# Three groups of the feed-forward stage normalised at the end of the scan, the steepness test moved, and an unread state half left out

## The reference

```python
xn = layernorm(x, ln_w, ln_b)
z, xBC, dt = split(xn @ in_proj_w)
xBC = silu(causal_conv1d(xBC, conv_w, conv_b))       # four taps
# state of each head: h = h * exp(dt * A) + dt * x * B ;  y = h . C
y = ssd_scan(xh, softplus(dt + dt_bias), Bm, Cm, -exp(A_log)) + D_skip * xh
y = y * silu(z)
y = y * rsqrt(mean(y * y) + 1e-5) * rms_w
out = y @ out_proj_w + x
h = relu(layernorm(out) @ mlp_w1 + mlp_b1) @ mlp_w2 + mlp_b2
out = h + out
# second layer: router softmax, two of 8 experts a token, a capacity for each expert,
# silu(x @ W1 + b1) @ W2 + b2, gated and added back, with layernorms and residuals around
```

## Time and profile before

| | us |
|---|---|
| median of 3 runs | 875.31 |
| lowest, highest | 872.54, 875.57 |
| profiled execution, its own time | 874.87 |
| its span | 873.1 |
| PE, DVE, ACT, POOL busy | 709.1, 608.5, 490.8, 441.3 |

### The profile page before, as it was taken

One profiled execution on the slowest core, in us unless ns is written; L12 is line 12 of the kernel. 1 busy time (PEld: TensorE's weight loads), 2 busy tenths in 40 slices (PEclk: granted clock), 3 DMA queues, 4 the chain that ended last, 5 costly groups with the idle time before them and its releaser, 6 DMA issues. The chain is left out here.

```text
span 873.1 us, 14642 instructions
## 1 busy us (share of the span) xinstructions
PE 709.1 (81%) x3872; PEld 492.4 (56%) x3872; DVE 608.5 (70%) x2176; ACT 490.8 (56%) x1209; POOL 441.3 (51%) x576
## 2 busy tenths in 40 slices
PE   7657999999999997999999840055698878879994
PEld 3325667777777775698989730023454444444542
DVE  7957999999999993799999888897111211121168
ACT  4864666666667675687877426334243432334257
POOL 7603767667667664233433530000757777777500
PEclk8877999999999998999999955555699998999997
DMA  9930000000000000600000004000322212221197
GB/s 220 382 132 20 1 2 2 2 1 1 2 1 2 2 2 9 186 1 2 2 2 1 2 0 196 0 0 8 94 64 72 75 50 74 75 75 47 40 355 223
DMA packets 50414, 52.92 MB, mean 61 GB/s; under 512 B 7576, under 2 KB 39624, under 8 KB 50080
## 3 DMA queue, kind: packets, MB, share of 16 engines
q1 hardware_dynamic: 44496, 41.62, 14.6%
q0 software_dynamic: 5120, 10.37, 4.2%
q10 hardware_dynamic: 720, 0.05, 0.1%
HBM read 28.04 MB, written 24.18 MB: 60 GB/s over the span
## 5 line engine op out<-in xcount | busy, mean ns | idle before, releaser
L917 DVE SCALAR_TENSOR_TENSOR s_cv<-s_pU,tap_w,s_cv 128x256 f32<-128x256 f32 x372 | 153.4, 477 | 11.1 <-ACT s_cv L848 10.7
L1939 POOL DMA_INDIRECT arena<-token_rows,token_of x80 | 81.1, 1014 | 115.3 <-issue 114.7
L2060 DVE TENSOR_TENSOR arena<-e_pB,e_gate 128x384 f32<-128x384 f32 (+2 forms) x24 | 14.5, 602 | 122.5 <-PE e_pB L1984 122.5
L1947 POOL DMA_INDIRECT choice_rows<-arena,choice_of x80 | 79.6, 995 | 32.9 <-issue 22.6
L2011 ACT ACTIVATE e_h<-e_pH,e_bcols 128x384 f32<-128x384 f32 (+2 forms) x96 | 58.7, 616 | 65.4 <-PE e_pH L1968 63.0
L1968 PE MATMUL e_pH<-e_xgT,e_w 128*128 128x384 f32 (+2 forms) x192 | 82.7, 580 | 0.0
L716 POOL TENSOR_TENSOR s_xa<-s_xt,arena 128x512 f32<-128x512 f32 x32 | 34.4, 1074 | 86.9 <-ACT s_xt L866 86.9
L848 ACT ACTIVATE s_cv<-s_pU,tap_b,tap_w 128x256 f32<-128x256 f32 x124 | 63.5, 560 | 23.3 <-PE s_pU L750 23.0
L750 PE MATMUL s_pU<-arena,w_in 128*128 128x262 f32 x248 | 68.2, 399 | 8.4 <-DVE s_cv L917 3.9
L1976 PE MATMUL e_pO<-e_h,e_w 128*128 128x384 f32 (+2 forms) x192 | 72.7, 522 | 0.4 <-ACT e_oT L2018 0.4
L1492 PE MATMUL m_pM<-w_m,m_h 128*128 128x128 f32 x512 | 62.7, 276 | 0.1
(11 more groups left out here) (308 smaller groups left out, 1874.3 us busy)
## 6 DMA issues: line engine op xcount, KB each, us to landing
choice_rows<-zrow SPq DMA_DIRECT2D x16, 512.0 KB, 8.4
arena<-choice_rows SPq DMA_DIRECT2D x28, 256.0 KB, 5.1
token_rows<-arena SPq DMA_DIRECT2D x8, 520.0 KB, 5.8
n_x<-in_L_attn_x_dram SPq DMA_DIRECT2D x8, 512.0 KB, 7.5
arena<-in_L_attn_x_dram SPq DMA_DIRECT2D x8, 512.0 KB, 4.7
e_w<-in_L_ffn_W_dram SPq DMA_DIRECT2D x16, 256.0 KB, 3.1
out_dram<-arena SPq DMA_DIRECT2D x14, 256.0 KB, 4.2
decay_rows<-arena SPq DMA_DIRECT2D x2, 1024.0 KB, 4.7
```

Of the source, the lines that this page charges most:

```text
L917: v.scalar_tensor_tensor(out=by_tile(cv[:, p % 2, m, :]), in0=columns(m)[:, :, tap:tap + P], scalar=tap_w[:, m, tap:tap + 1], in1=by_tile( ...
L1939: g.indirect_dma_start(xg[:, n % RING, i, :], None, table, bass.IndirectOffsetOnAxis(ap=token_of[:, c:c + 1], axis=0), bounds_check=TOKENS ...
L1947: g.indirect_dma_start(choice, bass.IndirectOffsetOnAxis(ap=choice_of[:, c:c + 1], axis=0), yo[:, n % RING, i, :], None, bounds_check=2 * ...
```

## The change

A class `Opening` holds the residual sum, the statistics, the roots and the normalisation for the first three groups (`READY = 3`) with semaphores of its own. Its parts are called from the scan's queues: on ACT at lags 2 and 4 of the last pair, on DVE behind the staged list. The exact scan runs the same parts again in a second block at its end, since it writes `proj` and `ssq` anew. In the feed-forward stage the functions for the first normalisation return at once for those groups, and their semaphores are advanced by three at the start. The buffers that both stages use (`root_y`, `sd_y`, `m_h0`, `m_stats`, `m_mv`, `m_sd`, `m_rs`) move into spare columns of the tile `cv`, and `m_hn` is allocated for the whole kernel. The transposition of the extremes and the comparison move into the last pair's step. `add_b` returns at once for the last four pairs, `states` leaves the second bank out for them, and for the last three `states` waits for `carry_b` in the place of `add_b`.

```diff
+            def roots(self, a):
+                a.activation(sd_y[:, 0:G * READY], ssq[:, 0:G * READY], ACT.Sqrt, bias=eps[:, 0:1], scale=1.0 / INNER).then_inc(self.root, 1)
+            def deviation(self, a, g):
+                need(a, self.var, g)
+                a.activation(m_sd[:, 0, g], m_mv[:, 0, g, :, 1], ACT.Sqrt, bias=eps[:, 0:1]).then_inc(self.sd, 1)
+            def invert_roots(self, v):
+                v.wait_ge(self.root, 1)
+                v.reciprocal(root_y[:, 0:G * READY], sd_y[:, 0:G * READY]).then_inc(self.inverse, 1)
+                v.wait_ge(self.inverse, 1)
+            def residual(self, v, g):
+                for i in range(G):
+                    t = G * g + i
+                    ins = v.scalar_tensor_tensor(out=m_h0[:, g, i, :], in0=proj[:, t, :], scalar=root_y[:, t:t + 1], in1=res[:, g, i, :],
+                                                 op0=ALU.mult, op1=ALU.add)
+                ins.then_inc(self.h0, 1)
+                need(v, self.h0, g)
+                for i in range(G):
+                    ins = v.bn_stats(m_stats[:, 0, g, i, :], m_h0[:, g, i, :])
+                ins.then_inc(self.stat, 1)
+                need(v, self.stat, g)
+                for i in range(G):
+                    ins = v.bn_aggr(m_mv[:, 0, g, i, :], m_stats[:, 0, g, i, :])
+                ins.then_inc(self.var, 1)
+            def normal(self, v, g):
+                need(v, self.sd, g)
+                v.reciprocal(m_rs[:, 0, g], m_sd[:, 0, g]).then_inc(self.rs, 1)
+                need(v, self.rs, g)
+                for i in range(G):
+                    ins = v.tensor_scalar(m_hn[:, g, i, :], m_h0[:, g, i, :], m_mv[:, 0, g, i, 0:1], m_rs[:, 0, g, i:i + 1],
+                                          ALU.subtract, ALU.mult)
+                ins.then_inc(self.hn, 1)
+            def vector(self, v):
+                self.invert_roots(v)
+                for g in range(READY):
+                    self.residual(v, g)
+                    if g:
+                        self.normal(v, g - 1)
+                self.normal(v, READY - 1)
...
                 def states(p):
                     need(pe, s_bt, p)
                     need(pe, s_xa, p)
-                    need(pe, s_st, p, 1)
+                    if p <= PAIRS - BACK:
+                        need(pe, s_st, p, 1)
+                    else:
+                        need(pe, s_sb, p, 1)
                     for t in range(G2):
-                        for c in range(2):
+                        for c in range(2 if p < PAIRS - BACK else 1):
...
+                def far_row(p):
+                    if p == PAIRS - 1:
+                        pe.wait_ge(s_all, 1)
+                        need(pe, s_bt, p)
+                        pe.transpose(pTr[0:1, 0:P], farther[:, :], ident[:, :]).then_inc(s_row, 1)
                 staged([(0, project(0)), (0, project(1)), (3, outputs), (1, gram), (1, turn_x), (0, project(2)), (0, project(3)),
-                        (2, states), (1, turn_b), (4, turn_out), (2, project_z), (4, out_project)])
-                pe.wait_ge(s_all, 1)
-                need(pe, s_bt, PAIRS - 1)
-                pe.transpose(pTr[0:1, 0:P], farther[:, :], ident[:, :]).then_inc(s_row, 1)
+                        (2, states), (1, turn_b), (2, far_row), (4, turn_out), (2, project_z), (4, out_project)])
...
-                staged([(0, first_tap(0)), (0, first_tap(1)), (1, silu_b), (1, silu_c), (5, projected), (1, silu_x), (0, first_tap(2)),
-                        (0, first_tap(3)), (1, silu_bt), (4, turned), (4, squares), (2, silu_z), (2, residual_first)])
+                # open_roots, open_first, open_others: for the last pair alone, roots(a), deviation(a, 0), deviation(a, 1 and 2)
+                staged([(0, first_tap(0)), (0, first_tap(1)), (1, silu_b), (1, silu_c), (5, projected), (4, open_first), (1, silu_x),
+                        (0, first_tap(2)), (0, first_tap(3)), (1, silu_bt), (4, turned), (4, squares), (4, open_others), (2, silu_z),
+                        (2, residual_first), (2, open_roots)])
...
                 def add_b(p):
+                    if p >= PAIRS - BACK:
+                        return
...
-                staged([(0, extremes_of), (0, taps(0)), (1, mask), (3, scaled), (0, taps(2)), (2, add_a), (2, carry_b), (2, add_b)])
-                v.wait_ge(s_row, 1)
-                v.tensor_reduce(farthest[0:1, :], pTr[0:1, 0:P], AX.X, ALU.max).then_inc(s_all, 1)
-                v.wait_ge(s_all, 2)
-                v.tensor_scalar(steep[0:1, :], farthest[0:1, :], STEEP, None, ALU.is_gt).then_inc(s_all, 1)
+                def compared(p):
+                    if p == PAIRS - 1:
+                        v.wait_ge(s_row, 1)
+                        v.tensor_reduce(farthest[0:1, :], pTr[0:1, 0:P], AX.X, ALU.max).then_inc(s_all, 1)
+                        v.wait_ge(s_all, 2)
+                        v.tensor_scalar(steep[0:1, :], farthest[0:1, :], STEEP, None, ALU.is_gt).then_inc(s_all, 1)
+                staged([(0, extremes_of), (0, taps(0)), (1, mask), (3, scaled), (0, taps(2)), (2, add_a), (2, carry_b), (2, add_b),
+                        (2, compared)])
+                need(v, s_bs, PAIRS - 1)
+                need(v, s_cs, PAIRS - 1)
+                need(v, s_bt, PAIRS - 1)
+                need(v, s_o, READY - 1)
+                opening.vector(v)
...
+            def opened(g):
+                return isinstance(g, int) and g < READY
...
                 a.activation(sd_y[:, :], ssq[:, :], ACT.Sqrt, bias=eps[:, 0:1], scale=1.0 / INNER).then_inc(s_extra2, 1)
+                a.sem_inc(s_sd[0], READY)
...
+                for s_ in (s_h0, s_st[0], s_var[0], s_rs[0], s_hn):
+                    v.sem_inc(s_, READY)
                 v.wait_ge(s_extra2, 1)
```

More of the change, by code:

```diff
@@ L196, in build @@
         rev, enough, base = taken(EXPERTS), taken(4), taken(1)
+        NB, G, READY = 4, 2, 3
+        root_y, sd_y = taken(TILES), taken(TILES)
+        m_stats = taken(3 * NB * G * 6).rearrange("p (n k g s) -> p n k g s", n=3, k=NB, g=G)
+        m_mv = taken(3 * NB * G * 2).rearrange("p (n k g s) -> p n k g s", n=3, k=NB, g=G)
+        m_sd, m_rs = (taken(3 * NB * G).rearrange("p (n k g) -> p n k g", n=3, k=NB) for _ in range(2))
+        assert room[0] <= 1024
+        m_h0 = spare_room[:, 1024:2048].rearrange("p (k g d) -> p k g d", k=NB, g=G)
+        m_hn = sb("m_hn", [P, NB, G, D])
         same_half = sb("c_same_half", [P, P], F16)
@@ L625, in _, with __init__ @@
                 v.memset(state[:, :, :], 0.0)
+        class Opening:
+            def __init__(self, name):
+                self.root, self.inverse, self.h0, self.stat, self.var, self.sd, self.rs, self.hn = (
+                    nc.alloc_semaphore(name=name + n) for n in ("_root", "_inverse", "_h0", "_stat", "_var", "_sd", "_rs", "_hn"))
+            def roots(self, a):
[36 more added lines that the diff above has]
+                self.normal(v, READY - 1)
@@ L628, in build @@
+        opening, opening_again = Opening("fast"), Opening("slow")
         with ExitStack() as st:
@@ L904, in residual_first, with open_roots, open_first, open_others @@
                         a.activation(res[:, q, i, :], x_first[:, t, :], ACT.Identity, bias=minus_m[:, t:t + 1], scale=rstd[:, t:t + 1])
-                staged([(0, first_tap(0)), (0, first_tap(1)), (1, silu_b), (1, silu_c), (5, projected), (1, silu_x), (0, first_tap(2)),
-                        (0, first_tap(3)), (1, silu_bt), (4, turned), (4, squares), (2, silu_z), (2, residual_first)])
+                def open_roots(p):
+                    if p == PAIRS - 1:
+                        opening.roots(a)
+                def open_first(p):
+                    if p == PAIRS - 1:
+                        opening.deviation(a, 0)
+                def open_others(p):
+                    if p == PAIRS - 1:
+                        for g in range(1, READY):
+                            opening.deviation(a, g)
+                staged([(0, first_tap(0)), (0, first_tap(1)), (1, silu_b), (1, silu_c), (5, projected), (4, open_first), (1, silu_x),
+                        (0, first_tap(2)), (0, first_tap(3)), (1, silu_bt), (4, turned), (4, squares), (4, open_others), (2, silu_z),
+                        (2, residual_first), (2, open_roots)])
             @block.vector
@@ L1162, in _ @@
                         v.tensor_tensor(mine, decayed[:, :], pS[:, INNER:2 * INNER], ALU.add).then_inc(s_done, 1)
+            with nc.Block() as block:
+                @block.scalar
+                def _(a):
+                    opening_again.roots(a)
+                    for g in range(READY):
+                        opening_again.deviation(a, g)
+                @block.vector
+                def _(v):
+                    opening_again.vector(v)
+            nc.all_engine_barrier()
         def choices(v, t, done, logits_ready):
@@ L1202, in build @@
             st.callback(stage_over)
-            NB, G = 4, 2
```

(12 more changed lines are left out.)

1 line of the change is left out of this document (added).

## The result

The changed kernel takes 880.22 us in the median of 6 runs (878.23 to 881.16); the kernel before took 875.44 beside it (872.54 to 876.55, 6 runs). The ratio is 1.0064, 95% interval 1.0048 to 1.008. The forecast was 875.5, its range ended at 877.6. A second series of the same kernel gave 878.47 against 874.64, 1.0051 [1.0031, 1.007].

What follows compares the result with a forecast made beforehand. Only moving the feed-forward stage's first real matmul or unloading its pacing engine counts; the filler stays. Scan end 345.3 instead of 345.12, +0.2 us, rest unchanged: 875.5 on the median's scale, range 872.4 to 877.6.

Steps and rivals of the forecast that it cites:

- The group price, "1.45 from residual to variance": Normalisation on DVE at the scan's end: each group takes 1.45 us from residual to variance, so DVE ends with ACT, 345.3.
- ACT's and PE's chain: Scan's drain: the root's table load delays PE's turns and projections, so ACT's last copy ends at 345.3 instead of 344.83.
- the rival of an earlier fall: Clock falls one stretch earlier in the drain, `out_project(30)` taking 2.08 instead of 1.16; +1.2 us, 876.7; chance 0.07.
- Also hidden: `deviation(1)` and `(2)` on ACT, after the squares near 343.6 and before the last copy at 344.95, add no time.
- The filler's 6.7 us: PE's five filler matmuls opening the feed-forward stage still take 6.7 us, so the first transpose comes at 354.0.
- The body jumped over grows by one block, which I cost at 0: Seam after the scan: one more block in the skipped exact scan costs 0 us.
- The end above, 1.99: Upper end for the larger skipped body: another 1.99 us at the seam between the scan and PE's filler.
- The four `add_b` and half a `states`: Last pairs of the scan: dropping `add_b` gains 0 of 2.76 us; half a `states` taken as 0, some 0.5 per pair at best.
- the drain: Rival: ACT's table switch at the scan's end also drains, putting +1.3 us on the chain; 876.8; chance 0.04.
- the reloads: Rival: Square is not in the root's table, so ACT reloads at 1.28 us a time; +4.6 us, 879.9; chance 0.04.
- DVE's lead of three groups: Rival: 6.5 us of three groups' work comes off DVE's pace in the feed-forward stage; 868.8; chance 0.05.
- The bound that I had set myself: Prediction is wrong as a whole if the first transpose moves over 2 us against the scan's last full pair.

Runs made afterwards that it cites:

- e2_own_root: Changed kernel with the root's tile first in its block, removing the 40 ns register instructions ahead of the loop's sums; 877.83 us, 1.0037 of before.
- e3_after_gates: Judging by its name, the changed kernel with DVE's opening waiting for POOL's last gated product; that run took 878.43 us, 1.0039 of before.
- e4_no_opening_barrier: Kernel before with only the moved test and unread half left out, plus a never-run block with one memset and a barrier; 875.49 us, 1.0023 of before.

## Why the prediction was wrong

*The group price, "1.45 from residual to variance".* This is the step that failed at the seam. The price was read at 349.13, in a stretch where POOL stood idle, and used for 338.4, where POOL makes the last pair's two products. The first pair of sums took 2.68 instead of 0.61, and DVE ended at 346.90 instead of 345.3. Of the 2.18 us by which the first transpose came later than the 354.0 foreseen, 0.25 lie ahead of the last `mask`, 1.35 are DVE's end, 0.13 the jump and 0.45 the filler. The rows of before would have shown it: POOL's `yg(31)` is the releaser of PE at 341.00, and the prediction used that very number on PE's side without asking what POOL's two operations do to DVE. The Trainium skill, "SBUF — State Buffer", section "Who interferes with whom", has the rule: a VectorE instruction with two SBUF inputs contends with a GpSimd instruction that reads SBUF, as its second input comes through a read interface that the two share, and the order of issue decides which of them blocks. The traces agree, with 0.61 alone and 2.68 beside 1.26 and 1.28 of POOL; POOL, which began 0.08 us earlier, lost nothing.

*ACT's and PE's chain.* Right in its order, short in size: `turn_out(30)` at 338.76 (338.55 foreseen), the last copy's end at 346.19 (345.3). The clock fell at 341.0, half a microsecond earlier, so the last transposes took 1.08 instead of 0.66. That is the rival of an earlier fall in part, with a later projection hit than it named; but it set nothing, since the copy ended at 346.06 in the second trace, where the clock held. "Also hidden" was wrong of `deviation(2)`: it was to come before the last copy at 344.95, and waited for DVE until 345.5.

*The filler's 6.7 us.* It took 7.16, with the clock back at 354.6. The term is not fixed: it was 5.83 to 7.27 in the traces of the kernels with five fillers and an opening of three groups. A fixed length was the wrong form for it.

*"The body jumped over grows by one block, which I cost at 0".* The second failed step. The end above, 1.99, was put on the seam's jump; the jump stayed (2.12), and the cost came 260 us later, at the first gather: 1.65 us in the changed kernel (4.04 against 2.39), 2.0 in the kernel without opening to which a block was added. The Trainium skill, "Runtime: NRT & Kernel Launch", section "Instruction fetch mechanics", says that the cost of crossing from one block of code to the next is mostly hidden. If the gap is such a crossing, which no run shows, the trace disagrees: 4.0 us against 2.0.

*Smaller terms.* "The scratch buffers' new places add no instruction" was wrong: in the loop a register instruction of 40 ns stands ahead of each residual sum. Without it groups 8 to 31 took 104.56 us in `e2_own_root` against 104.61, so it cost nothing.

*What held.* The four `add_b` and half a `states` brought no time that the traces show: the last `mask` starts 0.25 us later than before's, the last `scaled` 0.29 (337.85 against 337.56). One table load of 1.28 us and a root at 338.05: neither the drain nor the reloads came, and Square and Copy ran behind the root's load without another. That the time came out near the reloads' 879.9 is chance. The first transpose waited for the filler alone, and DVE's lead of three groups was not kept. The bound that I had set myself, 2 us for the first transpose against the last full pair, was passed: 29.63 us after the last `mask` instead of 27.52.

*What stays open.* Some 0.4 us in the changed kernel's loop (groups 8 to 31: 104.61 against 104.23) and 0.6 between its end and the token list. What makes a turn of that loop longer in some kernels, and the clock fall behind it, is open. What sets the filler's length, beyond the share of it at half clock, is open too. Which instruction is fetched where was not seen. A wait of 1.96 us at the loop's turn was followed by full clock in `e3_after_gates`, one of 1.53 by half clock in `e4_no_opening_barrier`; the length of the wait alone doesn't decide it.

## What to carry to other kernels

Before work is moved into an engine's idle time, read what the other engines do in that same stretch, above all GpSimd beside VectorE sums with two operands in SBUF; a duration is only good for the neighbours that it was measured with. Work that is moved ahead of a stage can't help where it ends after the last thing of the stage that it joins, or where something else (here the filler) holds the next start. A difference of 2 us far from the edit can be the place of code: compare with a version that has the same code and doesn't run it.

## What was not expected of the hardware

A block that is never executed cost 2.0 us at the first gather (1.98 to 3.97 us), and 8 memsets on an idle engine take as much back (4.04 to 2.01). Two executions of the changed kernel had their clock fall 7 us apart in the drain (341.0 and 348.0), and their first transposes started within 0.08 us of each other. Waits of 1.53 to 2.06 us at a loop turn were followed by half clock in five kernels, where the sixteen matmuls behind them took 2.83 to 3.49 us instead of 1.95; one of 1.96 in `e3_after_gates` was not.
